# Input-tile statistics moved in VectorE's order: three tiles a step in steps 0 to 9, at the end of the step

## What is computed

```python
x = x + tanh(g_xattn[0]) * xattn(_layernorm(x), ctx_1024, Wq, Wk, Wv, Wu, bu, qn_w, qn_b, kn_w, kn_b)
x = x + tanh(g_ffn[0])   * ffn(_layernorm(x), Wg, W1, b1, W2, b2, Ws1, bs1, Ws2, bs2)
# xattn: 16 heads of 64; q = emb @ Wq.T, k = ctx @ Wk.T, v = ctx @ Wv.T; q and k are layer-normed per head;
#        softmax(q k^T / 8) v, then @ Wu.T + bu
# ffn:   8 experts of 512 hidden units, the top 2 of them per token, and a shared expert times 0.1
# _layernorm(x): (x - mean) / sqrt(var + 1e-5) over the 128 features
```

## Time and profile before

| what | us |
|---|---|
| median of 3 runs (lowest, highest) | 649.66 (648.73, 649.98) |
| the profiled execution, its time | 648.96 |
| its span in the profile | 647.2 |
| TensorE busy | 589.9 (91%) |
| VectorE busy | 452.3 (70%) |
| ScalarE busy | 452.4 (70%) |
| GpSimd busy | 364.4 (56%) |
| mean granted clock of TensorE, of 1 | 0.979 |

### The profile page before, as it was taken

One profiled execution on the slowest core, in us unless ns is written; L12 is line 12 of the kernel. 1 busy time (PEld: TensorE's weight loads), 2 busy tenths in 40 slices (PEclk: granted clock), 3 DMA queues, 4 the chain that ended last, 5 costly groups with the idle time before them and its releaser, 6 DMA issues.

```text
span 647.2 us, 21127 instructions
## 1 busy us (share of the span) xinstructions
PE 589.9 (91%) x7726; PEld 523.1 (81%) x7726; DVE 452.3 (70%) x1032; ACT 452.4 (70%) x986; POOL 364.4 (56%) x711
## 2 busy tenths in 40 slices
PE   6989999999999999999999998897589999999994
PEld 5768888888788888777888776776489999999984
DVE  4788988988988878887887888427155544444427
ACT  3779998998888888788888777462335455455555
POOL 2545666756567677577767657547205555555520
PEclk9999999999999999999999999799599999999998
DMA  7900100200001110100200000011212222222247
GB/s 240 304 4 2 35 19 4 91 20 25 28 11 34 35 32 21 53 10 20 60 11 18 12 10 18 17 36 54 80 42 72 77 72 79 74 77 72 62 153 263
DMA packets 22581, 38.01 MB, mean 59 GB/s; under 512 B 5232, under 2 KB 13040, under 8 KB 22352
## 3 DMA queue, kind: packets, MB, share of 16 engines
q1 hardware_dynamic: 17648, 27.27, 13.7%
q0 software_dynamic: 4544, 9.38, 4.1%
q10 hardware_dynamic: 288, 0.00, 0.0%
HBM read 23.17 MB, written 13.47 MB: 57 GB/s over the span
## 4 chain that ended last, share of the span: by engine, by line
PE 69%; DVE 10%; issue 9%; ACT 4%; POOL 3%; DMA 2%; another core or an unknown queue 2%; POOLq 0%; DVEq 0%; ACTq 0%; SPq 0%
PE ps L1446 9%; PE ps L1193 7%; PE ps L1249 7%; PE ps L1219 7%; PE ps L1161 6%; PE ps L1163 5%; PE ps L1162 5%; PE ps L1202 4%; PE ps L1234 4%; PE ps L1330 3%; PE ps L1432 2%; PE ps L1430 2%; PE ps L1431 2%; DVE wide L823 2%; PE ps L1419 2%
## 5 line engine op out<-in xcount | busy, mean ns | idle before, releaser
L739 POOL DMA_INDIRECT results<-spo,xs_ix x78 | 75.2, 964 | 89.6 <-DVE spo L1117 72.9
L420 ACT ACTIVATE qk_T<-ps,lnw 128x512 f32<-128x512 f32 x128 | 96.7, 786 | 6.6 <-PE ps L1193 6.0
L1161 PE MATMUL ps<-w_hi,xc_hi 128*128 128x512 f32 x192 | 87.0, 453 | 5.1 <-DVE w_lo L759 3.0
L823 DVE TENSOR_TENSOR wide<-ps,rstd 128x512 f32<-128x512 f32 x128 | 87.3, 682 | 5.4 <-POOL rstd L654 5.3
L816 DVE TENSOR_REDUCE ss<-wide 128x16 f32<-128x1024 f32 x64 | 77.8, 1216 | 15.9 <-ACT wide L396 13.8
L1193 PE MATMUL ps<-ident,wide 128*128 128x128 f32 x512 | 78.4, 278 | 5.0 <-ACT row_T L472 2.9
L1446 PE MATMUL ps<-w_sb,qk_T 128*128 x624 | 76.7, 276 | 4.3 <-ACT qk_T L553 4.3
L553 ACT ACTIVATE qk_T<-ps,b_now 128x256 f32<-128x256 f32 x156 | 61.3, 482 | 25.0 <-remote 14.5
L1446 PEld LDWEIGHTS ps<-w_sb,qk_T 128*128 128x128 f32 x624 | 73.0, 192 | 5.9 <-issue 5.9
L396 ACT ACTIVATE wide<-ps 128x512 f32<-128x512 f32 x128 | 76.0, 595 | 1.6 <-PE ps L1163 1.6
L1193 PEld LDWEIGHTS ps<-ident,wide 128*128 128x128 f32 x512 | 58.7, 145 | 21.7 <-ACT spo L450 7.9
(11 more groups left out here) (187 smaller groups left out, 1379.0 us busy)
## 6 DMA issues: line engine op xcount, KB each, us to landing
v_sb<-routed SPq DMA_DIRECT2D x39, 130.0 KB
xc_in<-in_x SPq DMA_DIRECT2D x8, 256.0 KB, 3.0
xc_in<-in_ctx SPq DMA_DIRECT2D x8, 256.0 KB, 3.4
w_raw<-in_L_ffn_W SPq DMA_DIRECT2D x8, 256.0 KB, 2.6
out_x<-x_res SPq DMA_DIRECT2D x8, 256.0 KB, 3.5
x_res<-in_x SPq DMA_DIRECT2D x1, 1792.0 KB, 8.5
w_raw<-results SPq DMA_DIRECT2D x3, 512.0 KB, 4.7
rows_all<-results SPq DMA_DIRECT2D x3, 512.0 KB, 8.5
```

Of the source, the lines that this page charges most:

```text
L420: nc.scalar.activation(qk_T[:, n, 4 * j:4 * j + 4, :].rearrange("p a n -> p (a n)"), ps[6 + j][:, :], ACT.Identity, bias=lnw[:, 2 * n + 1: ...
L739: gp_.indirect_dma_start(out=results[:, :], out_offset=bass.IndirectOffsetOnAxis(ap=xs_ix[:, b4, a:a + 1], axis=0), in_=yb[:, b4, a, :], i ...
L823: nc.vector.tensor_tensor(qk_n[:, n, j * 512:(j + 1) * 512].rearrange("p (h d) -> p h d", h=8), ps[2 * n + j][:, :].rearrange("p (h d) -> ...
L1161: nc.tensor.matmul(out_bank, xc_hi[:, t % XD, src, :], w_hi[:, w, cols[j]], start=True, stop=False)
```

## The change

Three things. `token_statistics` leaves its place ahead of `second_statistics`, but for the steps before step 0 (tiles 0 to 2). In steps s >= 0 it is called three times, for tiles 3(s+1) to 3(s+1)+2, behind `keep_logits` and ahead of `route`, which is the end of VectorE's step. Tiles 3 to 31 are thus done in steps 0 to 9 (three each in steps 0 to 8, two in step 9), and no step from 10 on has any. For this, `mv` and `eps_q` get a column for each of the 32 tiles, and the two waits that kept the four columns apart go.

```diff
-        mv = sb("mv", [P, 4, 2])
-        eps_q = sb("eps_q", [P, 4])
+        mv = sb("mv", [P, TILES, 2])
+        eps_q = sb("eps_q", [P, TILES])
...
+        STATISTICS = 3
...
-            return eps_q[:, t % 4:t % 4 + 1] if n == 0 else eps[:, 1, 0:1]
+            return eps_q[:, t:t + 1] if n == 0 else eps[:, 1, 0:1]
...
-                    if t >= 4:
-                        gp_.wait_ge(rstd_ready[0], t - 3)
-                    nc.gpsimd.tensor_scalar(eps_of(0, t), mv[:, t % 4, 1:2], LN_EPS, LN_EPS, ALU.add, ALU.mult).then_inc(epsq_ready, 1)
+                    nc.gpsimd.tensor_scalar(eps_of(0, t), mv[:, t, 1:2], LN_EPS, LN_EPS, ALU.add, ALU.mult).then_inc(epsq_ready, 1)
...
-                    if t >= 4:
-                        ve.wait_ge(epsq_ready, t - 3)
-                    nc.vector.bn_aggr(mv[:, t % 4, :], bn6[:, :]).then_inc(mv_ready, 1)
+                    nc.vector.bn_aggr(mv[:, t, :], bn6[:, :]).then_inc(mv_ready, 1)
...
-                token_statistics(s + 3)
+                if s < 0:
+                    token_statistics(s + 3)
                 second_statistics(s - 2)
...
                 keep_logits(s - 4)
+                if s >= 0:
+                    for k in range(STATISTICS):
+                        token_statistics(STATISTICS * (s + 1) + k)
                 route(s, ROUTE_LAG)
```

## The result

| | before | after |
|---|---|---|
| median of the runs, us | 648.76 (648.14 to 649.98, 5 runs) | 657.43 (654.13 to 658.21, 5 runs) |
| ratio to before, 95% interval | | 1.013, 1.0101 to 1.016 |
| forecast, us | | 658.2 (655.5 to 660.3) |
| the profiled execution's span, us | 647.2 | 655.7 |
| from the first maximum of step 0 to that of step 10, us | 112.68 | 121.20 |

The kernel became 8.7 us slower, and the stretch in which the statistics now stand at the end of a step is 8.5 us longer. The median of the kernel before is 648.76 here, from five runs, where the three runs known to the forecast gave 649.66. The first two lines are the page's engine rows and the chain that ended last; they answer to the earlier trace rows. The last two come from the waits of the whole execution (total us, times, longest us).

A forecast was written before the change was run, and what follows sets the result against it. TensorE was taken to set the pace in most steps, with VectorE's loop taking over once its slack is used up. Terms 6.7 + 1.5 + 0.3 = 8.5 us on 648.96 gave 657.5, the median 0.7 higher: 658.2 us, range 655.5 to 660.3.

The forecast's parts named there:

- step 0: VectorE's loop has no slack in this step, so the added statistics cost their whole 1.42 + 0.08: +1.5 us.
- step 1: VectorE idles 0.95 ahead of the sum of squares; statistics fill it or it stays, 0 to 0.6, middle taken: +0.3 us.
- steps 2 to 9: Loop of 10.65 plus gaps of 1.42 to 1.49 (0.95 in step 9): 96.44 against 89.73, +6.7 us.
- later, up to the last maximum: The pair leaving ahead of the maximum only lengthens VectorE's idle time there, periods as before: 0 us.
- Loop plus gap: Period is VectorE's 10.65 us loop plus the gap from second subtraction's end to sum of squares, once slack is used up.
- The slack: Step 2, between GpSimd's product and TensorE's transposes of the probabilities: 0.38 us of room before the loop sets the period.
- rival C: Slack is larger or early stalls in steps 0 and 1 swallow step 0's 1.5 us: 656.7 us, chance 0.12.
- B: Pairs at the end of steps 0 to 9 follow at 0.10, not 0.22: 2.3 us less, 655.9, chance 0.11.
- D: ScalarE's logarithm, waiting for the late sum of squares, holds TensorE up 0.2 a step over ten steps: 660.2, chance 0.11.
- E: Not slower: the pair leaving ahead of the maximum wins 0.42 in each of steps 10 to 28: 650.2, chance 0.06.
- The signs: Profile after: periods 12.0 to 12.2 in steps 2 to 8, whole loss in steps 0 to 9, periods as before from 10.

The follow-up runs named there:

- the arrays alone: Only the 32-column mv and eps_q and the two dropped waits, statistics left at their old place, against the kernel before: 605.44 us, ratio 0.9999.
- set 3: Runs beside the kernel before (605.42 us): the changed kernel 1.0163, it with an unused pair ahead of the maximum 1.0166, more routing work moved 0.9943.
- set 2: Runs beside the kernel before (642.44 us): three unchained pairs 1.0064, an unused pair ahead of the maximum 1.016, routing spread 0.9899, that with statistics two a step 0.9929.
- the pair put back: Changed kernel plus an unused pair ahead of the maximum in steps 10 to 28: 652.17 us (1.016), later 615.58 (1.0166) beside the changed kernel's 615.52.
- set 1: Runs beside the kernel before (605.29 us): the changed kernel 1.0176, wider arrays and fewer waits only 0.9999, three pairs at the old place 1.0085, one at the end 1.0079.

## Why the prediction was right

**The size.** Forecast +8.5 us on the profiled execution, from step 0 to step 9; measured 121.20 - 112.68 = +8.52. The profiled execution was forecast at 657.5 and took 657.43. The median was forecast 0.7 higher, as in the kernel before with its three runs, and is 657.43 too. That the sum meets to the last digit is partly luck, as its terms show:

| term | forecast | measured |
|---|---|---|
| step 0 | +1.5 | 12.16 - 10.57 = +1.59 |
| step 1 | +0.3 | 12.10 - 12.38 = -0.28 |
| steps 2 to 9 | +6.7 | 96.94 - 89.73 = +7.21 |
| later, up to the last maximum | 0 | +1.2 |
| start of step 0 | 0 | +0.21 |
| behind the last maximum | 0 | -1.5 |

**Steps 2 to 9 (forecast 0.5 too small).** Loop plus gap held in each: 10.66 + 1.44 = 12.10, 10.66 + 1.51 = 12.17, 10.66 + 0.96 = 11.62. Half of what lacks is step 5, where the gap is 1.74, from an instruction that was left out of the sum, the clearing of `picked`, which stands behind the statistics there:

```profile
98.06 0.18 DVE L790 BATCH_NORM_AGGREGATE mv<-bn 128x2 f32<-128x6 f32 x1
98.20 0.06 DVE L959 MEMSET picked<- 128x4 uint32 x1
98.40 1.22 DVE L813 TENSOR_REDUCE ss<-wide 128x16 f32<-128x1024 f32 x1
```

That it is only 0.06 long and yet makes the gap 0.23 longer shows once more that the starts count, not the durations. In the kernel before its step had slack for it. The other half are 0.03 to 0.04 a step in the loop's length and the gap.

The slack was read too small. The forecast took 0.54 - 0.16 = 0.38 in step 2, but its own loop gives 11.04 - 10.57 = 0.47 there, and the run with one pair at the end fitted 0.42 into it. The sum didn't use the 0.38. Nor is a short way from product to transposes a sure sign that the gap sets the pace. In steps 6 and 7 of the kernel before it is 0.14, and yet the gap is -0.01 and the period 11.56 and 11.35, and one pair at the end costs nothing (11.58 and 11.37, as with the arrays alone). GpSimd has no idle time ahead of its work on the sum of squares there: it comes late by its own work.

**Step 1 (forecast +0.3, measured -0.3).** The term took VectorE's idle time in step 1 for a stall of its own that either stays or is filled. It comes from TensorE. This row of the kernel before shows it, and TensorE has no such pause there in the kernel after:

```profile
44.92 0.74 PE L1234 MATMUL ps<-spo,v_sb 64*64 64x64 f32 x34 [1.22 <-issue]
```

VectorE's gap in step 1 follows this pause: 1.22 with a pause of 1.49 (the arrays alone), 0.68 with 0.94 (three pairs at the old place). The pause comes at this very instruction, with 30 of 64 products done, and has many lengths. In profiles with step 0 as before or 0.4 longer it was 1.22, 1.49, 1.49, three times 0.94, and once absent. With step 0 longer by 0.8 to 2.8 it was 0.95, 1.37, 0.61, and three times absent. Where it is 0.95, step 1 takes 12.13: the statistics fill the idle time. Where it is 1.37, the step takes 12.53, still short of the 13.02 at the upper end of the term. A third case was missing, that the pause isn't there at all.

The traces' DMA packets tell what its length goes with. The page of the profile lists a queue q8 for instructions, with 64 packets of 16 KB in the span, one in some 10 us. In the kernel before, one of them ends at 43.55; the products behind the pause were due at 43.70 and start at 44.92, which is 1.37 behind its end. In steps 0 to 30 of all 13 profiles TensorE pauses 36 times for 0.5 us or more with "issue" as the reason. All 36 pauses stand at these attention products, and each ends 1.19 to 1.57 behind the end of a q8 packet. Where the pause of step 1 is absent, the packet had ended 1.5 to 2.7 before the products were due. So the pause is what is left, when the products are due, of some 1.3 to 1.5 us behind the packet, and packets this rare don't stand there by chance.

This answers rival C's question in part. In the kernel after, the packet came at the same time as in the kernel before (from 42.34, against 42.33), and the products 1.6 later, so the stall passed, as C had it; but the step then takes the 12.10 of the loop, so little of the time came back. In three other profiles with three chained pairs (two of set 3, one of set 2) the packet itself came 1.6 to 3.2 later, counted from the first maximum, and a pause stayed. Why the packet is late or not is open. Counting steps 0 and 1 together, the change cost 1.3 in the first comparison, where the forecast had 1.8 and rival C 0.3.

**Steps 10 and 12 (+0.94 and +0.59, not forecast).** The forecast's sign for them, periods as before and 12.07 in step 12, failed. Most of it comes from more pauses of this kind, here from the kernel after, in step 10 with 59 of 64 products done, and in step 12:

```profile
156.12 0.33 PE L1235 MATMUL ps<-spo,v_sb 64*64 64x64 f32 x5 [1.14 <-issue]
...
180.26 0.46 PE L1235 MATMUL ps<-spo,v_sb 64*64 64x64 f32 x15 [0.59 <-issue]
```

The kernel before has the first too, with 0.20:

```profile
146.45 0.34 PE L1234 MATMUL ps<-spo,v_sb 64*64 64x64 f32 x5 [0.20 <-issue]
```

At this instruction the pause is 0.59 and 1.14 in the two other profiles of the changed kernel, 0.46 to 1.14 in the five kernels that have its pairs in part or in another form, 0.20 and 0.67 in the two with only the routing spread, and absent in the one with the arrays alone and the one with the statistics two a step. So the change isn't needed for it, though the longest ones stand in kernels with three pairs. The DMA view of the 7 us around it shows nothing but two packets of the queues for instructions, 0.02 MB and 0.01 MB:

```profile
q8 instruction: 1, 0.02, 1.4%
```

The q8 packet ends at 154.82, the products are due at 154.98 and start 1.3 behind the packet. In the two kernels without a pause there, it had ended 1.3 and 1.6 before they were due. That fits a TensorE whose next instructions have yet to be fetched. It rests on times that go together in every profile, not on a run made to test it.

In step 12 there is something else besides. VectorE stands idle for 0.25 ahead of the sum of squares, behind the last instruction of its routing work:

```profile
184.07 1.22 DVE L813 TENSOR_REDUCE ss<-wide 128x16 f32<-128x1024 f32 x1 [0.25 <-issue]
```

This row is in all three profiles of the changed kernel and in the one with three pairs at the old place, and in none of the other nine. In sets 1 and 3, without a pause of TensorE in step 12, the step takes 12.43 and 12.44 with it, and 12.10 with the arrays alone. So some 0.3 of the loss in step 12 comes with the change every time; why is open. The changed kernel's step 10 measured 12.54, 12.56 and 12.01 against 11.60 and 11.34, so 0.4 to 1.2 us of its loss lie there, on top of the loop.

**Behind the last maximum (-1.5).** In the profile of before the granted clock drops there, in that of after it doesn't. The 16 products of `wu` show it, first before, then after:

```profile
411.18 3.64 PE L1249 MATMUL ps<-wu_sb,spo 128*128 128x128 f32 x16
```

```profile
420.84 1.95 PE L1250 MATMUL ps<-wu_sb,spo 128*128 128x128 f32 x16
```

That is 3.64 - 1.95 = 1.7 us which the profiled execution before had lost there. In the seven profiles of sets 1 and 3, with and without the statistics moved, the clock doesn't fall there and the stretch from the last maximum to the end takes 212.9 to 213.5, so the change gains nothing in it. In set 2 the clock fell there in three profiles and not in the one with three chained pairs; whether the change has a part in that isn't shown. The forecast had no such term. The forecast of the end was right by two errors that cancel: the pauses and the later start added 1.5 over the forecast, and the clock gave 1.5 back.

**The rivals.** B (cheaper pairs, 655.9) fell: the chained pairs start 0.22 apart again (72.61 + 0.22 = 72.83), and only with the chain cut is a pair cheaper. C is taken up under step 1. D (ScalarE blocks more) fell: GpSimd waits 1.98 and ScalarE 0.99 for the late sum of squares, and the transposes still follow the product by 0.14, with a period 0.03 longer than that of step 12. E fell by the pair put back.

**The signs.** Periods of 12.0 to 12.2 held in steps 2 to 8 but for step 5. The transposes 0.16 behind the product held (0.14). GpSimd's idle time ahead of the late sum of squares grew by 1.5 in steps 2 to 5 and 8; in steps 6 and 7, where GpSimd is late by itself, by 0.2 at most. The idle time before the maximum 0.42 longer from step 10 on held (0.70 against 0.29 in step 11). That steps 0 to 9 hold the whole loss did not: 1.2 us more arise up to the last maximum, mostly in steps 10 and 12.

## What to carry to other kernels

- Price an instruction on an engine off the critical path by the loop that it stands in: measure the loop's length without the gap in a step in which the loop already sets the pace, add the new gap, and compare with the period. Here 10.66 + gap met the periods with gaps of -0.08, 0.74, 0.96, 1.44, 1.65 and 1.74 within 0.02, in steps 0 to 12. It doesn't hold where another part of the loop is longer: in step 0 with the clock down (13.31), in steps 6 and 7 of the kernel before, and from step 13 on. The same pair cost 0 or up to 0.4 according to the step.
- Each place takes small work for nothing up to what it has: the idle time ahead of the loop's first instruction (0.3 to 0.6 us in steps 2 to 13 of the kernel before), and between two links of the loop the slack of the step, 0.5 to 0.6 where TensorE sets the pace and none where the loop does. One pair a step fitted into each. Moving half of the routing work ahead of the maximum, in steps where the loop sets the pace, won 1%. Packing three pairs into each of ten steps, at a place with slack for one, lost 1.3 to 1.8%.
- If short instructions must stand on such a path, let none wait for the one just before it: three pairs in the order stats, stats, stats, aggregate, aggregate, aggregate took half of the gap (0.74 against 1.43).

## What the runs showed of the hardware that was not expected

**Chained short instructions.** `bn_aggr` to a `bn_stats` that waits for it is 0.22 from start to start; three `bn_aggr` in a row that wait only for instructions long done take 0.30 in all, some 0.07 from start to start. Cutting the chain brought the ratio from 1.016 to 1.0064 in one set, some 6 us. By the Trainium skill, "VectorE: DVE Perf Modes", section "The DRAIN you can't avoid", a semaphore between chained instructions costs nothing extra, which was measured there on eight copies; for instructions as short as these the runs disagree (a `bn_stats` starts 0.22 behind a `bn_aggr` that it waits for, and 0.10 behind one that it doesn't).

**The clock after a longer wait.** After 2.3 us of idle time in step 0, TensorE was granted 0.50 for some 3 us in three of five profiled executions, and 1.00 in the other two. A wait of the same length came with 1.15 us more in one execution and nothing in the next.

**A pause behind a packet of instructions.** All 36 pauses of TensorE of 0.5 us and more that are put down to issue, in the attention steps of 13 profiles, end 1.19 to 1.57 us behind the end of a 16 KB packet of queue q8.

**The same program in different sets.** The kernel before took 605.3, 605.4, 642.4 and 648.8 us in the four comparisons, and two of them (605.4 and 642.4) ran on the same chip. The mean granted clock of the profiles differs by 2% at most (0.979 in that of before, 0.995 with the arrays alone in set 1). Up to step 12 the steps are alike. Some 18 of the 44 us arise before the last maximum: a step without routing work takes 11.99 from step 16 on in the slower case, and 11.15 in the faster. In the slower case TensorE pauses twice within the 64 score products, while GpSimd issues transfers with scattered rows. The kernel before in the first comparison, in step 15:

```profile
204.12 0.81 PE L1219 MATMUL ps<-qk_T 64*64 64x64 f32 x38
204.55 0.96 POOL L680 DMA_INDIRECT routed<-rows_all,slot  x1 [0.30 <-issue]
205.18 0.30 PE L1219 MATMUL ps<-qk_T 64*64 64x64 f32 x3 [0.26 <-issue]
205.94 0.56 PE L1219 MATMUL ps<-qk_T 64*64 64x64 f32 x20 [0.45 <-issue]
```

and the kernel with the arrays alone, at the same place in set 1, where the 64 run through:

```profile
203.59 1.16 PE L1216 MATMUL ps<-qk_T 64*64 64x64 f32 x64
204.02 0.96 POOL L679 DMA_INDIRECT routed<-rows_all,slot  x1 [0.30 <-issue]
```

The other 25 us lie behind the last maximum (238.65 against 213.15). Two differences show there. TensorE stands idle for 20.6 us against 4.9, of which 11.9 against nothing is put down to issue, most of it ahead of the products of L1330 and with no packet of q8 near. And the granted clock is 0.50 for 6.8 and for 13.7 us in the slower profile and 1.00 in the faster one, but for the very end in both. Which of the two comes first, and the cause of both, are open. It matters for the reading: the changed kernel lost 8.7, 11.0 and 10.1 us in its three comparisons, but what was won by moving routing work was 1.0% in the slower set and 0.6% in a faster one, with different amounts moved.
